# Adding four tiles' normalised rows to the output by DMA at the end of an attention and mixture-of-experts layer

## What is computed

```python
x = x + _layernorm(attn(_layernorm(x), W_qkv, W_proj))     # 16 heads, causal
x = x + _layernorm(ffn(_layernorm(x), gate_w, w_gate, w_up, w_down))

def ffn(h):                      # 16 experts, 6 per token
    scores = softmax(h @ gate_w.T)
    topk_w, topk_idx = top_k(scores, 6)
    for e in range(16):
        y += cw[:, e] * ((silu(h @ w_gate[e].T) * (h @ w_up[e].T)) @ w_down[e].T)

def _layernorm(x):               # no gain, no bias
    return (x - mean(x)) / sqrt(var(x) + 1e-5)
```

## Time and profile before

| what | value |
|---|---|
| time, median of 3 runs | 1682.74 us (1682.65 to 1682.80) |
| time of the profiled execution | 1683.45 us |
| span of the profiled execution, first to last instruction | 1681.3 us |
| TensorE busy | 1609.8 us (96%) |
| VectorE busy | 1189.7 us (71%) |
| ScalarE busy | 1146.0 us (68%) |
| GpSimd busy | 907.0 us (54%) |
| mean granted TensorE clock | 0.983 of full speed |

### The profile page before, as it was taken

How to read it: one execution, slowest core, us unless ns; L and a number is a source line. 1 busy time by engine, 2 the same in 40 slices (tenths; PEclk the granted TensorE clock), 3 DMA queues, 4 the chain that set the end, 5 groups by cost and what they waited for, 6 DMA issues and landing times.

```text
span 1681.3 us, 30901 instructions
## 1 busy us (share of the span) xinstructions
PE 1609.8 (96%) x9214; PEld 1360.1 (81%) x9214; DVE 1189.7 (71%) x2394; ACT 1146.0 (68%) x1729; POOL 907.0 (54%) x761
## 2 busy tenths in 40 slices
PE   7999999999999999999977999999999999999991
PEld 7988777777777777776756999999999999999991
DVE  6427888888888888887787667566665566556555
ACT  3222899999989999986776566566665565556554
POOL 2321788888888887874663443434343434343432
PEclk9999999999999999999988999999999999999996
DMA  8676221111111122212716898888887887788747
GB/s 254 188 222 186 63 67 51 50 50 50 50 50 50 51 71 71 59 48 88 267 48 237 234 283 243 230 257 237 240 254 216 223 259 213 205 253 235 195 111 219
DMA packets 103474, 268.21 MB, mean 160 GB/s; under 512 B 21129, under 2 KB 38921, under 8 KB 96073
## 3 DMA queue, kind: packets, MB, share of 16 engines
q1 hardware_dynamic: 77929, 204.64, 36.8%
q0 software_dynamic: 25440, 62.27, 18.2%
HBM read 190.55 MB, written 59.27 MB: 149 GB/s over the span
## 4 chain that ended last, share of the span: by engine, by line
PE 86%; DVE 6%; DMA 3%; issue 2%; ACT 1%; POOL 1%; SPq 1%; DVEq 0%; ACTq 0%; POOLq 0%
PE p_prj L91 26%; PE a_op L893 13%; PE a_sp L911 8%; PE a_mp L852 8%; PE p_at_ps L91 7%; PE p_logit_ps L91 7%; PE e_qp L91 5%; PE p_ht_ps L2031 3%; PE p_at_ps L2054 2%; PE e_vp L91 2%; PE a_op L884 2%; PE a_mp L855 1%; PE a_sp L915 1%; PE a_shared L870 1%; DVE r_lane_hot L1718 1%
## 5 line engine op out<-in xcount | busy, mean ns | idle before, releaser
L717 POOL TENSOR_TENSOR prob_lo<-prob,prob_hi 128x1024 fp32r<-128x1024 f32 (+1 forms) x211 | 467.0, 2245 | 120.5 <-DVE prob_hi L796 119.4
L767 DVE TENSOR_REDUCE part_max<-a_mp 128x1 f32<-128x512 f32 (+2 forms) x600 | 358.8, 609 | 79.5 <-PE a_mp L852 48.1
L1428 POOL DMA_INDIRECT acc_rows<-m_y_out,m_row_ids x108 | 175.2, 1622 | 401.2 <-ACT m_y_out L1587 254.3
L752 ACT ACTIVATE prob<-a_sp 128x1024 f32<-128x1024 f32 x320 | 292.5, 926 | 13.2 <-PE a_sp L911 10.7
L91 PE MATMUL p_prj<-m_w_hi,m_ht_hi 128*128 128x352 f32 x888 | 297.5, 335 | 1.8 <-DVE m_ht_lo L1827 1.5
L91 PE MATMUL p_prj<-m_w_lo,m_ht_hi 128*128 128x352 f32 x888 | 288.1, 324 | 0.0
L91 PE MATMUL p_prj<-m_w_hi,m_ht_lo 128*128 128x352 f32 x888 | 287.5, 324 | 0.0
L1851 DVE TENSOR_TENSOR m_w_lo<-m_w_raw,m_w_hi 128x704 fp32r<-128x704 f32 (+1 forms) x357 | 270.7, 797 | 23.4 <-ACT m_w_hi L1593 23.0
L739 ACT ACTIVATE prob_hi<-prob 128x1024 fp32r<-128x1024 f32 (+1 forms) x261 | 251.2, 962 | 8.3
L1593 ACT ACTIVATE m_w_hi<-m_w_raw 128x704 fp32r<-128x704 f32 (+1 forms) x357 | 229.0, 714 | 19.3 <-PE p_prj L91 16.8
L1837 DVE TENSOR_TENSOR m_at_lo<-p_at_ps,m_at_hi 128x384 fp32r<-128x384 f32 x111 | 61.8, 557 | 252.4 <-ACT m_at_hi L1579 252.4
(11 more groups left out here) (259 smaller groups left out, 3245.4 us busy)
## 6 DMA issues: line engine op xcount, KB each, us to landing
m_w_raw<-wexp SPq DMA_DIRECT2D x51, 1408.0 KB, 7.0
m_w_raw<-wexp SPq DMA_DIRECT2D x51, 768.0 KB, 5.9
qk_parts<-rows SPq DMA_DIRECT2D x64, 256.0 KB, 3.2
multi<-qk_parts SPq DMA_DIRECT2D x84, 128.0 KB, 2.9
v_head<-v_all SPq DMA_DIRECT2D x16, 520.0 KB, 3.6
k_stack<-qk_parts SPq DMA_DIRECT2D x42, 128.0 KB, 2.6
q_stack<-qk_parts SPq DMA_DIRECT2D x42, 128.0 KB, 2.8
m_w_raw<-wexp SPq DMA_DIRECT2D x2, 2176.0 KB, 12.2
```

Of the source, the lines that this page charges most:

```text
L717: nc.gpsimd.tensor_tensor(prob_lo[:, t % RING, :, c0:NB], prob[:, t % RING, :, c0:NB], f32(prob_hi[:, t % RING, :, c0:NB]), ALU.subtract). ...
L752: nc.scalar.activation(prob[:, t % RING, :, c0:NB], sp_[:, t % 2, :, c0:NB], ACT.Exp, scale=SCALE).then_inc(prob_ready, 1)
L767: nc.vector.reduce_max(part_max[:, qb, kb:kb + 1], mp[:, n % 2, 0:width], AX_X).then_inc(piece_done, 1)
L1428: nc.gpsimd.indirect_dma_start(acc_dram, bass.IndirectOffsetOnAxis(ap=row_id(t), axis=0), y_out[:, t % 4, :], None, compute_op=ALU.add).th ...
```

## The change

Group 3, tiles 8 to 11, takes another way to the output. In the expert stage, with blocks 6 to 9, SyncE's queue stores `rows` of these four tiles to the output. At the end ScalarE makes the whole normalised value in place in one instruction for each tile, with a scale (the inverse deviation) and a bias (minus the mean times the inverse deviation, `shift`, made by GpSimd in one small multiplication). GpSimd then adds each tile to the rows already in the output with an indirect DMA whose row numbers come from a new table, `token_id`, made by one iota in the projection stage. VectorE leaves these four tiles out. In ScalarE's program the statistics of tile 12 now come ahead of the four scaled tiles. In GpSimd's program the four adds come after the last of the five powers.

```diff
+ADDED_BY_DMA = 3
...
+        token_id, shift = sb("m_token_id", [P, NT], I32), sb("m_shift", [P, 4, 1], F32)
+        by_dma = range(*GROUPS[ADDED_BY_DMA])
...
                     load_down(b + 2, e)
+                if b - 2 * FORCED in range(len(by_dma)):
+                    t = by_dma[b - 2 * FORCED]
+                    sp.dma_start(out_dram[t], rows[:, t, :]).then_inc(rows_out, 16)
...
-            for t in range(NT):
-                sp.wait_ge(out_ready, t + 1)
+            by_dve = [t for t in range(NT) if t not in by_dma]
+            for n, t in enumerate(by_dve):
+                sp.wait_ge(out_ready, n + 1)
                 sp.dma_start(out_dram[t], rows[:, t, :]).then_inc(out_stored, 16)
-            sp.wait_ge(out_stored, 16 * NT)
+            sp.wait_ge(out_stored, 16 * len(by_dve))
+            sp.wait_ge(rows_added, 16 * len(by_dma))
...
+                pool.wait_ge(made, CONSTANTS)
+                nc.gpsimd.iota(token_id[:], pattern=[[P, NT]], base=0, channel_multiplier=1).then_inc(token_ids_made, 1)
...
+                if g == ADDED_BY_DMA:
+                    pool.wait_ge(rstd_done, g + 1)
+                    nc.gpsimd.tensor_tensor(shift[:], minus[:, lo:hi], rstd[:, lo:hi], ALU.mult).then_inc(shift_done, 1)
+            pool.wait_ge(rows_out, 16 * len(by_dma))
+            pool.wait_ge(token_ids_made, 1)
+            for n, t in enumerate(by_dma):
+                pool.wait_ge(scaled, n + 1)
+                nc.gpsimd.indirect_dma_start(out_rows, bass.IndirectOffsetOnAxis(ap=token_id[:, t:t + 1], axis=0),
+                                             final_tile(t), None, compute_op=ALU.add).then_inc(rows_added, 16)
...
+            for g, (lo, hi) in enumerate(GROUPS):
+                if g != ADDED_BY_DMA + 1:
+                    statistics(lo, hi)
+                if g == ADDED_BY_DMA:
+                    statistics(*GROUPS[g + 1])
+                    act.wait_ge(shift_done, 1)
+                    for t in by_dma:
+                        nc.scalar.activation(final_tile(t), final_tile(t), ACT.Identity, bias=shift[:, t - lo],
+                                             scale=rstd[:, t, 0:1]).then_inc(scaled, 1)
+                    continue
                 act.wait_ge(veps_done, g + 1)
...
                 for t in range(lo, hi):
-                    dve.wait_ge(centred, t + 1)
+                    if t in by_dma:
+                        continue
+                    dve.wait_ge(centred, t + 1 - sum(s < t for s in by_dma))
```

More of the change, by code:

```diff
@@ L1093, in shared_space, with layer_stage @@
     return small, [ctx.enter_context(nc.sbuf_tensor(*one)) for one in big]
-def layer_stage(nc, embed, attend, attended, x_dram, wproj_landed, w_dram, h_dram, acc_dram, list_dram, chosen_dram, out_dram, rows, flat, ident, ln_consts):
+def layer_stage(nc, embed, attend, attended, x_dram, wproj_landed, w_dram, h_dram, acc_dram, list_dram, chosen_dram, out_rows, out_dram, rows, flat, ident, ln_consts):
     with ExitStack() as ctx:
@@ L1195, in layer_stage @@
         out_ready, out_stored = sem("m_out_ready"), sem("m_out_stored")
+        rows_out, scaled, rows_added, shift_done = sem("m_rows_out"), sem("m_scaled"), sem("m_rows_added"), sem("m_shift_done")
+        token_ids_made = sem("m_token_ids_made")
+        token_id, shift = sb("m_token_id", [P, NT], I32), sb("m_shift", [P, 4, 1], F32)
+        by_dma = range(*GROUPS[ADDED_BY_DMA])
         prob_ready, pv_done, rows_stored = attended
@@ L1608, in _, with statistics @@
             weigh(TILES - 1)
-            for g, (lo, hi) in enumerate(GROUPS):
+            def statistics(lo, hi):
                 for t in range(lo, hi):
@@ L2121, in build_layer @@
                                                       early_landed, head0_max_landed, masks, flat, wproj, wgate, wproj_landed)
-        layer_stage(nc, embed, attend, attended, x_tiles, wproj_landed, wexp, h_dram, acc_dram, list_dram, chosen_dram, out_tiles, rows, flat, ident, ln_consts)
+        layer_stage(nc, embed, attend, attended, x_tiles, wproj_landed, wexp, h_dram, acc_dram, list_dram, chosen_dram, out, out_tiles, rows, flat, ident, ln_consts)
 def kernel(L0_attn_x, L0_attn_W_qkv, L0_attn_W_proj, L0_ffn_gate_w, L0_ffn_w_gate, L0_ffn_w_up, L0_ffn_w_down):
```

## The result

The changed kernel takes 1689.21 us, median of 6 runs (1688.38 to 1691.38), against 1682.70 of the kernel before (6 runs): a ratio of 1.0039, 95% interval 1.0027 to 1.0051. It is 6.5 us slower. The forecast was 1687.0, 4.3 us slower, with a range of 1684.6 to 1689.8.

The account below looks back on a forecast made before the run. Bound: matmuls (TensorE 96% busy), then VectorE's tiles at the end. The last power to 1674.5, four spaced adds, a 4.8 landing and 0.4 ending give span 1685.6, 4.3 longer: 1687.0 us; range 1684.6 to 1689.8.

Parts of the forecast that it names:

- the early stores: SyncE's four stores in blocks 6 to 9: costed at nothing, hidden by TensorE; rival, 8%: one late weight load, 2.2 us.
- VectorE's gain of 2.6 us: Four line 1892 instructions leave VectorE, 2.6 us; waiting for centred tile 12 cuts this to 0.9, ending at 1677.8.
- the adds set the end: At the kernel's end the four adds finish last, 4.3 us after the old end, so VectorE's gain does not count.
- GpSimd shut out: Rival, 10%: add issues cannot proceed beside VectorE's last four two-input instructions, 2.75 us on top, 1689.8.
- Cheap issues: Rival, 12%: adds over rows in order issue like gathers, every 1.25 us, giving 1684.6, not measurably slower.
- The sum for the rest: From the end of VectorE's last statistics, 1673.4, to the end of the span, 1685.6: 12.2 us.
- The landing of the last add: Last of GpSimd's four adds lands 4.8 us after its issue starts, as the last scatters do, at 1685.2.
- The spacing: GpSimd's four adds start every 1.87 us, from 1674.8 to 1680.4, priced from the scatter of line 1428.
- The start: First add starts 0.3 us behind GpSimd's last power, which ends at 1674.5, so at 1674.8.
- The ending: After the last add's landing at 1685.2, 0.4 us of ending follow to the span's end, 1685.6.

Follow-up runs that it names:

- the kernel with two tiles: Changed kernel with only tiles 8 and 9 added by plain DMA, the first ahead of GpSimd's last power, the second behind it: 1686.51 us, ratio 1.0018.
- the indirect add ahead of the power: Changed kernel with the first of its four indirect adds moved ahead of GpSimd's last power: 1688.87 us in one execution.
- the lone add: Changed kernel with only tile 8's indirect add, issued once all stores to the output have landed; tiles 9 to 11 not added: 1690.27 us, one execution.
- The four plain adds: Changed kernel with plain adding DMAs from GpSimd, rows in order, in place of the four indirect ones: 1688.13 us, ratio 1.0032.

## Why the prediction was right, and what it missed

The main line held. The matmuls and the stretch before the last scatter did not care, the early stores were hidden (0.9997), VectorE's gain of 2.6 us shrank to 1.1 (predicted 0.9; its end came 4.2 us after its statistics, predicted 4.4), and the adds set the end. The sign is right. The size is right only in part. The forecast was 4.3 us slower and the measurement 6.5; 1689.21 lies outside the forecast's own range of 1685.4 to 1688.6, and inside the stated range of 1684.6 to 1689.8 only because that had been widened for rivals. The rival next to it, GpSimd shut out (1689.8), did not come in its size, so that the stated range held is in part luck. The profiled execution flatters the forecast too, 1688.38 against 1687.75: it was 1.8 us ahead of the old one before the end began.

The shut-out rival was right in kind and not in size: VectorE does hold up an issue, by 0.5 us, once, not by its whole 2.75. The prediction itself had bounded such a loss at 0.5 an issue from the longest scatter. The Trainium skill, SBUF — State Buffer, section "Who interferes with whom", calls the sharing of VectorE's second pair of ports with GpSimd an exclusive lock and infers that descriptor generation is spared by `tensor_tensor` with both inputs in SBUF. The kernel's instruction is `scalar_tensor_tensor`, with two inputs in SBUF as well, and for it the trace does not agree: the issue took 2.08 us beside it and 1.61 without it. Cheap issues did not come: indirect adds over rows in order cost 1.54, as scatters do.

The sum for the rest was 2.8 us short (12.2 against 15.0), and four terms of it were mis-sized:

- *The landing of the last add*, taken as 4.8 us because the last scatters had nothing else in the DMA engines: measured 6.2. This is the largest miss, 1.4. What the term left out first is that adds in a row stand behind each other. A lone one lands in 4.6, the last of four without stores or VectorE in 6.0, the last of four with them in 6.2. By the record each of four adds alone takes 2.1 us of all 16 engines, 0.2 more than their spacing, which makes 0.7 over three spacings. That is an estimate from the queue's row and accounts for half of the 1.4 between 4.6 and 6.0; the other half stays open.
- *The spacing*, predicted 3 x 1.87 = 5.6, measured 1679.13 - 1672.97 = 6.2: the first issue was 0.5 longer, beside VectorE.
- *The start*: the first add stands 0.56 and not 0.30 behind the power, 0.3 us. The gap is there with VectorE idle as well.
- *The ending* after the last landing was 1.0 us (1686.3 - 1685.3) and not 0.4, 0.6 us. SyncE's wait at the end for TensorE's queue is 0.5 to 0.6 us in all kernels whose last landing is an add's, and 0.2 in all others. Why was not found.

I had taken the landing from the old kernel's engines at rest and named the last stores as the neighbours; for the last add the neighbours that mattered most were the other adds.

## What to carry to other kernels

A DMA that adds is not a free add. It takes more than twice the DMA engines' time of a plain store of the same bytes (152 against 404 GB/s with the engines full here), plus an issue of 1 to 1.6 us on GpSimd. At the end of a kernel, where stores follow each other at the pace of the DMA engines, most of it comes out at the end: 1.2 us for one add here. Before work is moved from an engine to the DMAs, count the DMA engines in that stretch as an engine of their own, and put the last landing, not the last instruction, in the sum. Where an engine stands idle, letting it do the addition in its own way and storing once gave an end 1.5 us shorter in the profile than the same addition by DMA.

## What the runs showed of the hardware that was not expected

- GpSimd starts a DMA late when it had to wait: 1.1 us after the scaled tile in the kernel with two tiles, 0.46 for the indirect add ahead of the power, and 1.7 us after the last store's landing (1681.16) for the lone add, while an ordinary addition in the same place starts 0.08 us after its releaser. In the chain of the kernel with the lone add:

```profile
1681.24 0.04 POOLq L1469
1681.29 1.32 issue
1682.61 1.84 POOLq L1100
```

- A DMA issue on GpSimd may also slow VectorE; one execution shows it. While the early indirect add was issued (1672.90 to 1674.51), two small VectorE instructions, of lines 1919 and 1920, took 0.42 and 0.35 us, where the same ones took 0.17 and 0.16 in the kernel before and in the changed one.
- Records of GpSimd instructions beside a DMA issue overlap it, so their durations read too long. The power behind the early indirect add has 1.52 us in its row, but only 1.08 lie behind the issue's end, as in a power by itself (1.01 to 1.11 for four columns most often). Behind the plain add of the kernel with two tiles 1.6 of 1.91 us lie behind the issue's end; why that one was slow was not tested. The four plain adds, too, have durations that grow with their number, 0.97 to 1.84 us, while they start 0.6 us apart.
